# Late key/value units at the start of a causal attention stage, the next stage's first unit at its end, and logits placed behind the values

## The chip, the cores and the metric

One core of a Trainium2 chip runs the whole kernel. The metric is the device time of one execution in microseconds (us). TensorE (PE) multiplies matrices, VectorE (DVE), ScalarE (ACT) and GpSimd (POOL) do the rest, and SyncE (SP) starts most DMAs. Each engine works through its own instructions in program order and waits on semaphores.

## The reference

The kernel computes a two-layer decoder on x of shape (32, 128, 256) with a context of the same shape. Each sublayer is followed by a residual and a layer norm.

```python
x = _layernorm(x + _L0_attn_ref(x, ...))              # gated linear recurrence
x = _layernorm(x + _L0_xattn_ref(x, ctx_1024, ctx_1024, Wq, Wk, Wv))   # retention, decay mask
x = _layernorm(x + _L0_ffn_ref(x, wg, w1, b1, w2, b2))   # 8 experts, top 2, capacity
x = _layernorm(x + _L1_attn_ref(x, wq, wk, wv, wo))      # causal attention, 2 heads, rope
x = _layernorm(x + _L1_xattn_ref(x, ctx_1024, mask, ...))  # 16 heads over ctx, key mask
x = _layernorm(x + _L1_ffn_ref(x, hasher_w, keys, values_down, values_up, scale))
```

The last attention needs `K = ctx @ Wk + bk` and `V = ctx @ Wv + bv` of all 32 sequences. The router of the expert layer needs `logits = xt @ wg` of all tokens before any expert starts.

## The kernel before, in words

The 32 sequences are worked in 16 units of two (`UNITS` = 16, T = 256 tokens). The program is a row of stages. In each stage every engine runs the same `step(t)`, and `t.at(k, UNITS)` gives the unit that is k steps behind, so one step works on several units at different depths. The order of work on an engine is thus written out by hand in `step`. `pipelined` peels the first and last steps and loops the ones in between; its argument `first` names the first step that runs.

- **Stage A** (`a_tensor`, `a_scalar`, `a_vector`, `a_gpsimd`, `a_sync`; steps 0 to 20): recurrence, retention and router logits. In a step TensorE does, among others, the scaled scores' product with the values (line 673, which waits for VectorE's line 833), the query projection (622), the transposes of x2 (495), the logits (690, from the copy x2F that ScalarE makes in line 758), the values projection of the unit two steps younger (698) and the transposes of the context (495). The transposed context of each unit is stored in `cF_d`.
- **Router and early keys/values** (`kv_project`, `r_vector`): keys and values of units 0 to 8 (`KV_FIRST` = 9) are projected while VectorE computes the routing.
- **Stage M** (`m_*`; 16 tiles of 512 slots): the experts. It starts with gathers of token rows by GpSimd (line 1159). At its end `run_layer` closes the block: all engines meet at a barrier, after `m_end` on SyncE has waited for the last store of y.
- **Late keys/values** (`kv_rest_tensor`, `kv_rest_scalar`, lines 1353 to 1376): units 9 to 15 (`KV_REST` = 7). SyncE loads their seven context tiles after the barrier (1357); TensorE projects keys (line 503, 8 matmuls) and values (line 511, 8 matmuls) of each; ScalarE copies both banks out (1373) and starts the store into `kv_d` (1376). All that stands ahead of step 0 or step 2 of the next stage on TensorE and ScalarE, and TensorE then waits until the last copy is done.
- **Stage C** (`c_tensor`, `c_scalar`, `c_vector`, `c_gpsimd`, `c_sync`; steps 0 to 20): causal attention. GpSimd gathers four blocks of expert rows a unit (1432); VectorE mixes them with x2 and takes statistics (1617, 455); GpSimd takes the root (1412); ScalarE writes x3 (1421). TensorE turns x3 in step u+2 (495), projects queries (1472), keys (1472) and values (1527), makes the scores in step u+3 (1498, 1504), and in step u+4 transposes the probabilities (1486), multiplies with the values (1519) and projects out (1535). SyncE loads the key mask (line 1392) in step 0, and the first two units of stage E in step 16.
- **Stage E** (`e_*`; steps 0 to 17): sixteen-head attention. For the unit one step behind, `scores_and_less` makes two quads of scores at a time (1855, 1868), `less_max` takes their maxima on VectorE (2051), `turn_max` turns these (1888), and then the same scores are made again, transposed and with the maximum subtracted (1862, 1877), for `exps` on ScalarE (1968). `e_turn` and `e_query` (495, 503) and `e_keys` (1825, four copies on ScalarE) prepare a unit. Unit 0's turn and query stand in step 18 of stage C, its keys in step 19. Its scores come in stage E's step 1, and step 2 is the first with all parts.
- **Stage D**: the last feed-forward part, untouched.

## Time and profile before

| | us |
|---|---|
| median of 3 runs | 1602.99 (1600.58 to 1610.22) |
| the profiled execution, its own time | 1600.43 |
| its span in the trace | 1598.7 |

The profile is of one execution. The page gives each engine's busy share of the span: PE 93%, DVE 70%, ACT 51%, POOL 37%. Times in rows are microseconds from the start of the span. "PEclk" is the granted TensorE clock as a share of full speed (1.00 is 2.4 GHz, 0.50 is 1.2 GHz). In a timeline row the first number is the start, the second the duration; "x8" is eight instructions merged; what stands in brackets is the idle time of that engine before the row and what ended it. The stages lie at: A 0 to 250, router 250 to 299, M 299 to 677, late keys/values 683 to 713, C 713 to 910, E 910 to 1165, D from there.

### The profile page before, as it was taken

The page shows a single profiled execution, that of the slowest core. Times are in us where ns is not written, and L with a number is a line of the kernel's source. Part 1 is how long each engine was busy: PE and PEld are TensorE (multiplying, and loading weights), DVE is VectorE, ACT ScalarE, POOL GpSimd, SP SyncE. Part 2 cuts the span into 40 slices and gives each one's busy share as a digit, 9 for nine tenths or more (in the row PEclk, how much of TensorE's full clock was granted, in tenths as well). Part 3 has the DMA queues.
Part 4 walks back from the last instruction along what each step waited for, and adds up shares of the span by engine and source line. Part 5 has one row for each costly group of instructions (what it writes and reads, how often), then busy time and mean ns, then how long its engine had stood idle before and what let it go on. Part 6 is the DMA issues. An engine that isn't in the chain of part 4 may idle for free.

```text
span 1598.7 us, 34301 instructions
## 1 busy us (share of the span) xinstructions
PE 1479.5 (93%) x12682; PEld 1332.2 (83%) x12682; DVE 1113.4 (70%) x2303; ACT 819.1 (51%) x1559; POOL 583.5 (37%) x684
## 2 busy tenths in 40 slices
PE   5889989899999999978999799999979999999997
PEld 3777877799999999867778678888879999989997
DVE  3899988646655655317888468888767676868684
ACT  6777742344543454325777556656534444444442
POOL 2655540312111210037887213313124444444443
PEclk9999999899999999988999889999989999999999
DMA  6222253221323321062333124222136445454633
GB/s 209 73 80 79 72 184 132 68 74 57 104 95 105 105 95 38 14 220 76 91 94 108 59 92 134 82 66 70 36 78 126 103 101 114 91 117 85 127 77 67
DMA packets 118151, 151.97 MB, mean 95 GB/s; under 512 B 10090, under 2 KB 102852, under 8 KB 117508
## 3 DMA queue, kind: packets, MB, share of 16 engines
q1 hardware_dynamic: 110068, 127.48, 28.9%
q0 software_dynamic: 6560, 19.02, 4.2%
q10 hardware_dynamic: 1392, 3.70, 0.6%
q8 instruction: 85, 1.39, 0.4%
q14 instruction: 46, 0.38, 0.1%
HBM read 111.37 MB, written 38.80 MB: 94 GB/s over the span
## 4 chain that ended last, share of the span: by engine, by line
PE 31%; DVE 8%; issue 6%; DMA 5%; POOL 3%; ACT 2%; SPq 1%; DVEq 0%; POOLq 0%; ACTq 0%
PE psum L536 10%; PE psum L1900 4%; DMA arena_x<-wT_d 3%; PE psum L503 3%; PE psum L511 3%; PE psum L1877 2%; PE psum L1868 2%; DVE psum L2487 2%; PE psum L1472 2%; POOL arena_y L1432 1%; PE psum L1855 1%; PE psum L1862 1%; DMA wT_d<-arena_w 1%; SPq L2231 1%; PE psum L495 1%
## 5 line engine op out<-in xcount | busy, mean ns | idle before, releaser
L2258 POOL TENSOR_TENSOR d_g_parts<-arena_w,d_g_parts 128x512 fp32r<-128x512 f32 x128 | 166.5, 1301 | 241.4 <-ACT d_g_parts L2390 236.3
L536 PE MATMUL psum<-d_v_high,d_g_parts 128*128 128x256 f32 x1024 | 205.3, 284 | 4.8 <-POOL d_g_parts L2258 2.4
L536 PE MATMUL psum<-d_x_parts,d_v_high 128*128 128x256 f32 x1024 | 193.7, 287 | 1.3 <-DVE d_x_parts L531 1.3
L536 PE MATMUL psum<-m_w_high,m_h_parts 128*128 128x256 f32 x1024 | 188.0, 285 | 0.0
L1231 ACT ACTIVATE arena_x<-psum,b_e 128x512 f32<-128x512 f32 x128 | 88.3, 690 | 189.8 <-PE psum L536 88.8
L1159 POOL DMA_INDIRECT arena_x<-x_d,slot_row x64 | 66.7, 1043 | 293.6 <-PE psum L1205 229.4
L536 PEld LDWEIGHTS psum<-d_v_high,d_g_parts 128*128 128x128 f32 x1024 | 168.5, 192 | 5.9 <-issue 4.6
L536 PEld LDWEIGHTS psum<-d_x_parts,d_v_high 128*128 128x128 f32 x1024 | 159.3, 192 | 8.2 <-DVE arena_w L2493 5.3
L536 PE MATMUL psum<-m_xF_parts,m_w_high 128*128 128x512 f32 x512 | 159.9, 394 | 2.1 <-DVE m_xF_parts L531 2.1
L536 PEld LDWEIGHTS psum<-m_w_high,m_h_parts 128*128 128x128 f32 x1024 | 160.9, 192 | 0.0
L536 PE MATMUL psum<-d_vu_low,d_g_parts 128*128 128x256 f32 x512 | 145.4, 284 | 0.0
L536 PE MATMUL psum<-m_w_low,m_h_parts 128*128 128x256 f32 x512 | 145.1, 283 | 0.0
L536 PE MATMUL psum<-d_x_parts,d_vd_low 128*128 128x256 f32 x512 | 144.9, 283 | 0.0
L2398 ACT ACTIVATE arena_y<-psum 128x512 f32<-128x512 f32 x128 | 75.9, 593 | 119.6 <-PE psum L536 118.5
L2487 DVE SCALAR_TENSOR_TENSOR psum<-arena_y,psum 128x512 f32<-128x512 f32 x128 | 88.3, 690 | 68.8 <-ACT arena_y L2398 68.5
L2390 ACT ACTIVATE d_g_parts<-arena_w 128x512 fp32r<-128x512 f32 x128 | 80.5, 629 | 106.0 <-DVE arena_w L2493 106.0
L2493 DVE TENSOR_TENSOR arena_w<-psum,arena_x 128x512 f32<-128x512 f32 x128 | 88.5, 691 | 38.2 <-DMA arena_x<-wT_d 33.7
L531 DVE TENSOR_TENSOR m_h_parts<-arena_x,m_h_parts 128x512 fp32r<-128x512 f32 x128 | 84.7, 688 | 43.2 <-ACT m_h_parts L1235 43.2
L536 PEld LDWEIGHTS psum<-m_xF_parts,m_w_high 128*128 128x128 f32 x512 | 96.2, 190 | 21.7 <-issue 2.5
L1968 ACT ACTIVATE arena_x<-psum,arena_x 128x1024 f32<-128x1024 f32 x64 | 71.2, 1112 | 58.4 <-PE psum L1877 56.2
L536 PE MATMUL psum<-m_xF_parts,m_w_low 128*128 128x512 f32 x256 | 100.5, 393 | 0.0
L536 PEld LDWEIGHTS psum<-m_w_low,m_h_parts 128*128 128x128 f32 x512 | 98.4, 192 | 0.0
(284 smaller groups left out, 3699.3 us busy)
## 6 DMA issues: line engine op xcount, KB each, us to landing
arena_x<-wT_d SPq DMA_DIRECT2D x128, 256.0 KB, 5.7
arena_y<-in_L_ffn_w SPq DMA_DIRECT2D x16, 1024.0 KB, 8.0
x_d<-arena_x SPq DMA_DIRECT2D x32, 256.0 KB, 2.2
y_d<-arena_x SPq DMA_DIRECT2D x16, 512.0 KB, 9.0
arena_x<-kv_d SPq DMA_DIRECT2D x16, 512.0 KB, 3.5
kv_d<-arena_x SPq DMA_DIRECT2D x9, 512.0 KB, 2.8
arena_x<-in_x SPq DMA_DIRECT2D x16, 256.0 KB, 2.9
arena_x<-in_ctx SPq DMA_DIRECT2D x16, 256.0 KB, 3.1
```

What stands on the lines that cost most here:

```text
L503: ins = nc.tensor.matmul(dst[:, m * T:(m + 1) * T], w[name][:, c, m * P:(m + 1) * P], src[:, c, :], start=(c == 0), stop=(c == NC_ - 1))
L531: return nc.vector.tensor_tensor(dst, src, high.bitcast(F32), ALU.subtract)
L536: ins = nc.tensor.matmul(dst, left[a_], right[b_], start=start and k == 0, stop=stop and k == 2, skip_group_check=True)
L1159: nc.gpsimd.indirect_dma_start(out=M["x"][:, u.p, q, :], out_offset=None, in_=x2_d.rearrange("b s d -> (b s) d"), in_offset=bass.IndirectO ...
L1231: nc.scalar.activation(M["hr"][:, m % 4, :], bank(2 + m % 4), ACT.Relu, bias=b1_e[:, (u.c // 2) % 2, m:m + 1]).then_inc(m_hs, 1)
L1900: ins = nc.tensor.matmul(bank(7)[32 * quad:32 * quad + 32, (kind * NC_ + c) * S:(kind * NC_ + c + 1) * S], left, X["eT"][:, b, at:at + S], ...
L1968: nc.scalar.activation(X["eT"][:, b, half * 1024:(half + 1) * 1024].rearrange("p (q n) -> p q n", q=2), psum[:, 4:6, :], ACT.Exp, scale=HD ...
L2258: nc.gpsimd.tensor_tensor(K["gP"][:, s % 4, 1], K["g"][:, s % 2], K["gP"][:, s % 4, 0].bitcast(F32), ALU.subtract).then_inc(d_gl, 1)
L2390: nc.scalar.activation(K["gP"][:, s % 4, 0], K["g"][:, s % 2], ACT.Copy).then_inc(d_gh, 1)
L2398: nc.scalar.activation(K["th"][:, s % 2], bank(2 + s % 4).rearrange("p (k t) -> p k t", k=2), ACT.Tanh, scale=0.5).then_inc(d_th, 1)
L2487: nc.vector.scalar_tensor_tensor(z, K["th"][:, s % 2].rearrange("p k t -> p (k t)"), 1.0, z, ALU.add, ALU.mult).then_inc(d_t, 1)
L2493: nc.vector.tensor_tensor(K["g"][:, s % 2], z, K["w"][:, s // 4, 2 * (s % 4):2 * (s % 4) + 2, :] .rearrange("p k t -> p (k t)"), ALU.mult) ...
```

## The change

**Logits behind the values.** In stage A's step TensorE now does the values (698) between the transposes of x2 and the logits (690); ScalarE copies the values out before the logits.

**Kept context tiles.** At the end of the router's part SyncE loads the seven context tiles into memory that stage M doesn't use (four places of the weights that only stage A needs, and three at the ends of two arenas). After stage M's last tile and ahead of the barrier TensorE makes the first three of the 14 halves (a half is the keys or the values of a unit: 8 matmuls and one bank).

**Late units spread over stage C's first steps.** TensorE makes halves 3 to 9 before the steps, 10 and 11 at the start of step 3, 12 and 13 in step 4. ScalarE copies halves 0 to 5 out first, 6 to 9 at the start of step 2 (behind step 1's x3 of unit 0), 10 and 11 in step 3, 12 and 13 in step 4, and starts one store at the head of each of steps 2 to 7, the seventh in step 7. The key mask is loaded in step 2 instead of step 0.

**Stage E's steps 0 and 1 in stage C's last steps.** Unit 0's turn, query and keys move to step 17, its scores to steps 18 and 19, as do the turn, query and keys of unit 1 and the turn of unit 2; stage E then begins at its step 2 (`first=2`). The helpers `scores_and_less`, `turn_max`, `values`, `exps`, `less_rows`, `less_max` and the values' preparation (now `e_values`) become functions of the stage, otherwise as they were.

```diff
@@ a_tensor @@
+                if u3:
+                    done(pe, a_r2, u3.back(1))
...
+                    ins.then_inc(a_v, 1)
+                if u5:
                     done(pe, a_x2F, u5)
                     if u4:
                         done(pe, a_sc, u4)
@@ a_scalar @@
+                if u3:
+                    done(act, a_v, u3)
+                    done(act, a_ret, u3.back(2))
+                    nc.scalar.activation(A["v"][:, u3.p], seqs(bank(6)), ACT.Copy).then_inc(a_vs, 1)
                 if u5:
                     done(act, a_logit, u5)
@@ r_sync @@
+            for s in (a_gate, a_q, a_k, a_v, a_r2, a_ret, a_sc):
+                sp.wait_ge(s, UNITS)
+            sp.wait_ge(ln2[3], UNITS)
+            for k in range(KV_KEPT):
+                sp.dma_start(cF_kept[k].rearrange("p c t -> p (c t)"), cF_d[KV_FIRST + k]).then_inc(kv_kept, 16)
@@ m_tensor @@
             pipelined(pe, TILES, 1, step, unroll=4, peel=4)
+            pe.wait_ge(kv_kept, 16 * KV_KEPT)
+            pe.wait_ge(m_hh, TILES * HC)
+            project_features(bank(2), "L1_xattn_Wk", cF_kept[0])
+            project_rows(bank(3), "L1_xattn_Wv", cF_kept[0])
+            project_features(bank(4), "L1_xattn_Wk", cF_kept[1])
@@ late units @@
+        HALF_BANK = (2, 3, 4, 5, 6, 7, 4, 5, 6, 7, 5, 6, 7, 6)
+        HALVES_MADE = 3
+        def kv_rest_tensor(pe, *halves):
+            for n in halves:
+                k, j = divmod(n, 2)
+                src = cF_kept[k]
+                if HALF_BANK[n] in HALF_BANK[:n]:
+                    pe.wait_ge(kr_s, max(m for m in range(n) if HALF_BANK[m] == HALF_BANK[n]) + 1)
...
+        def kv_rest_scalar(act, *halves):
...
+                nc.scalar.activation(KV["kv_rest"][:, k, j], bank(HALF_BANK[n]), ACT.Copy).then_inc(kr_s, 1)
@@ c_sync @@
-                if t.fixed and t.n < 2:
-                    for k in ((0, 1), range(2, KV_REST))[t.n]:
-                        kv_rest_load(sp, k)
...
-                if t.fixed and t.n == 0:
+                if t.fixed and t.n == 2:
                     sp.dma_start(X["mask_u8"], a["mask"].rearrange("(a b) s -> a (b s)", a=1)
...
+                if t.fixed and t.n == UNITS + 3:
+                    e_load(sp, D2)
@@ c_tensor @@
-            kv_rest_tensor(pe)
+            kv_rest_tensor(pe, *range(3, 10))
...
+                if t.fixed and t.n == 3:
+                    kv_rest_tensor(pe, 10, 11)
...
+                if t.fixed and t.n == 4:
+                    kv_rest_tensor(pe, 12, 13)
+                    pe.wait_ge(kr_s, 11)
...
+                if t.fixed and t.n == UNITS + 2:
+                    pe.wait_ge(x_one, 6)
+                    for part in (c_x3F, c_qt, c_q2):
+                        pe.wait_ge(part, UNITS)
+                    done(pe, x_qs, D0)
+                    done(pe, x_ks, D0, 4)
+                    done(pe, x_mask, D0)
+                    scores_and_less(pe, (D0, 0, 0), None)
...
+                if t.fixed and t.n == UNITS + 1:
+                    e_turn(pe, D0, 0)
+                if t.fixed and t.n == UNITS + 3:
+                    scores_and_less(pe, (D0, 1, 0), None)
...
+                if t.fixed and t.n == UNITS + 2:
+                    for part in (c_kt, c_k2, c_vs):
+                        pe.wait_ge(part, UNITS)
+                    scores_and_less(pe, (D0, 0, 1), None)
+                if t.fixed and t.n == UNITS + 3:
+                    for part in (c_ex, c_pTs):
+                        pe.wait_ge(part, UNITS)
+                    scores_and_less(pe, (D0, 1, 1), (D0, 0, 0))
...
+                if t.fixed and t.n == UNITS + 1:
+                    e_query(pe, D0, 0)
                 if t.fixed and t.n == UNITS + 2:
-                    e_query(pe, Unit(0, 0, 4), 1)
+                    e_turn(pe, D1, 6)
+                    turn_max(pe, D0, 0)
+                if t.fixed and t.n == UNITS + 3:
+                    e_query(pe, D1, 6)
+                    turn_max(pe, D0, 1)
+                    done(pe, x_qs, D1)
+                    e_turn(pe, D2, 6)
@@ c_scalar @@
-            kv_rest_scalar(act)
+            kv_rest_scalar(act, *range(6))
...
+                if t.fixed and 2 <= t.n < 8:
+                    kv_rest_store(act, t.n - 2)
+                if t.fixed and t.n == 2:
+                    kv_rest_scalar(act, 6, 7, 8, 9)
...
+                if t.fixed and t.n == UNITS + 3:
+                    done(act, x_mkey, D0)
+                    exps(act, D0, 0, 0)
+                    e_take_query(act, D1, 6)
+                    e_take_turned(act, D2, 6)
+                    less_rows(act, D0, 1)
+                    e_keys(act, D1)
...
+                if t.fixed and t.n == UNITS + 1:
+                    e_take_query(act, D0, 0)
+                    e_keys(act, D0)
                 if t.fixed and t.n == UNITS + 2:
-                    e_take_query(act, Unit(0, 0, 4), 1)
-                if t.fixed and t.n == UNITS + 3:
-                    e_keys(act, Unit(0, 0, 4))
+                    e_take_turned(act, D1, 6)
+                    less_rows(act, D0, 0)
@@ c_vector (constants of stage E one step earlier, maxima and values of unit 0) @@
+                if t.fixed and t.n == UNITS + 2:
+                    less_max(dve, D0, 0, 0)
...
+                    e_values(dve, D0)
+                if t.fixed and t.n == UNITS + 2:
+                    less_max(dve, D0, 0, 1)
+                if t.fixed and t.n == UNITS + 3:
+                    less_max(dve, D0, 1, 0)
+                    less_max(dve, D0, 1, 1)
+                    e_values(dve, D1)
@@ e_sync, e_gpsimd, e_tensor, e_scalar, e_vector @@
-            pipelined(pe, UNITS, E_LAG, step, unroll=4, peel=4, tail=E_TAIL)
+            pipelined(pe, UNITS, E_LAG, step, unroll=4, peel=4, tail=E_TAIL, first=2)
```

## Rows read from the trace of the kernel before

**Rows 1.** Windows by stage: engines' busy us (instructions), then PEclk, DMA share, GB/s

```profile
60.00:210.00 150.00, 135.88 (x782) 119.92 (x782) 142.09 (x304) 116.42 (x210) 87.83 (x92) 1.00 0.29 93
...
677.30:715.20 37.90, 26.30 (x114) 22.62 (x113) 4.32 (x14) 8.69 (x16) 11.21 (x20) 0.86 0.63 220
715.20:747.60 32.40, 27.73 (x123) 23.01 (x124) 24.06 (x57) 15.62 (x42) 22.73 (x29) 0.84 0.24 75
747.60:880.80 133.20, 123.20 (x685) 105.78 (x684) 118.75 (x336) 98.62 (x263) 104.42 (x149) 1.00 0.34 99
880.80:928.00 47.20, 35.70 (x205) 28.63 (x203) 22.84 (x59) 25.22 (x65) 13.60 (x27) 0.83 0.13 45
```

**Rows 2.** Timeline of TensorE from stage M's end to stage C's step 5

```profile
677.03 0.28 PE L536 MATMUL psum<-m_w_high,m_h_parts 128*128 128x256 f32 x1
686.15 3.78 PE L503 MATMUL psum<-arena_x,arena_w 128*128 128x256 f32 x8 [8.84 <-DMA arena_x<-cF_d]
...
710.53 1.89 PE L511 MATMUL psum<-arena_w,arena_x 128*128 128x256 f32 x8
...
...
747.57 0.60 PE L495 MATMUL psum<-arena_w,arena_y 128*128 128x128 f32 x4
```

**Rows 3.** Timelines of GpSimd, VectorE and ScalarE between stages M and C

```profile
687.77 0.95 POOL L1432 DMA_INDIRECT arena_y<-y_d,c_idx_t  x1 [0.30 <-issue]
695.07 1.80 DVE L1617 SCALAR_TENSOR_TENSOR arena_y<-arena_y,gates 128x256 f32<-128x256 f32 x4 [16.43 <-DMA arena_y<-y_d,c_idx_t]
712.46 1.09 ACT L1373 ACTIVATE arena_x<-psum 128x512 f32<-128x512 f32 x2 [2.37 <-PE psum L511]
713.95 1.09 ACT L1421 ACTIVATE arena_y<-arena_y,C_st 128x256 f32<-128x256 f32 x2 [0.40 <-ACT arena_x L1373]
```

**Rows 4.** DMA view, issues by line: count, (KB,) median us to landing, 684 to 695

```profile
arena_y<-y_d,c_idx_t POOLq DMA_INDIRECT x5, 6.9
```

**Rows 5.** DMA view, 296 to 297 and 293 to 299, and TensorE's start of stage M

```profile
q1 hardware_dynamic: 79, 0.32, 102.4%
...
arena_x<-x_d,slot_row POOLq DMA_INDIRECT x5, 3.0
...
299.01 1.94 PE L1205 MATMUL psum<-arena_w,arena_x 128*128 128x128 f32 x8 [5.42 <-DMA arena_x<-x_d,slot_row]
```

**Rows 6.** Stage A: TensorE's wait for x2F (total, times, longest), then timeline rows

```profile
PE psum L690 <- ACT arena_x L758: 11.7, 16, 0.8
...
154.40 1.13 PE L673 MATMUL psum<-arena_x,arena_y 128*128 128x256 f32 x4 [0.76 <-DVE arena_y L833]
...
165.10 0.69 DVE L828 TENSOR_TENSOR arena_x<-arena_x 128x508 f32<-128x508 f32 x1
...
165.53 1.38 POOL L888 TENSOR_TENSOR arena_x<-arena_x 128x512 f32<-128x512 f32 x1 [3.82 <-ACT arena_x L729]
...
167.05 0.69 DVE L790 TENSOR_TENSOR arena_x<-psum,arena_w 128x512 f32<-128x512 f32 x1 [0.92 <-PE psum L622]
...
178.12 1.63 DVE L828 TENSOR_TENSOR arena_x<-arena_x 128x508 f32<-128x508 f32 x1
...
180.14 1.13 PE L673 MATMUL psum<-arena_x,arena_y 128*128 128x256 f32 x4 [0.77 <-DVE arena_y L833]
```

**Rows 7.** Timelines of TensorE and ScalarE from stage C's step 17 to stage E's step 3

```profile
890.65 1.89 PE L1535 MATMUL psum<-arena_w,arena_y 128*128 128x256 f32 x8
...
906.50 2.06 ACT L1825 ACTIVATE arena_x<-arena_x,kb_par,arena_w 128x256 f32<-128x256 f32 x4
...
911.91 1.04 PE L1868 MATMUL psum<-arena_x 32*128 32x256 f32 x8
...
927.99 0.61 PE L1855 MATMUL psum<-arena_x,mask_one 1*128 1x512 bf16 x2 [0.31 <-ACT arena_x L1968]
...
930.85 2.66 PE L503 MATMUL psum<-arena_x,L_xattn_Wq 128*128 128x256 f32 x8
...
945.66 1.99 PE L503 MATMUL psum<-arena_x,L_xattn_Wq 128*128 128x256 f32 x8
```

More of the change, by code:

```diff
@@ L693, in step @@
                     ins.then_inc(a_logit, 1)
-                if u3:
-                    done(pe, a_r2, u3.back(1))
-                    for b in range(UB):
-                        for c in range(NC_):
-                            ins = nc.tensor.matmul(bank(6)[:, b * D:(b + 1) * D],
-                                                   A["cF"][:, u3.p, c, b * S:(b + 1) * S],
-                                                   w["L0_xattn_Wv"][:, c, :], start=(c == 0), stop=(c == NC_ - 1))
-                    ins.then_inc(a_v, 1)
                 if u2:
@@ L1053, in decoder @@
         KV_FIRST = 9
+        KV_KEPT = UNITS - KV_FIRST
+        cF_kept = [w["L0_xattn_W" + n] for n in ("q", "k", "v")]
+        cF_kept.append(gate_w[:, :, :, :].rearrange("p g c n -> p g (c n)"))
+        arena_y.reset(13440)
+        cF_kept += [arena_y.take([P, NC_, T]) for _ in range(2)]
+        arena_x.reset(22528)
+        cF_kept.append(arena_x.take([P, NC_, T]))
+        kv_kept = sem("kv_kept")
         def kv_load(sp, u):
@@ L1516, in step @@
                     done(pe, c_os, u3.back(1))
+                    if t.fixed and t.n == UNITS + 3:
+                        done(pe, x_xF, D1)
+                    if t.fixed and t.n == 4:
+                        pe.wait_ge(kr_s, 2 * KV_REST)
                     for b in range(UB):
@@ new lines, in scores_and_less @@
+                            ins = nc.tensor.matmul(bank(4 + quad % 2)[:, j * S:(j + 1) * S],
+                                                   X["k"][rows, v.p, par, c * T + vb * S:c * T + (vb + 1) * S],
+                                                   X["q"][rows, v.c % 4, c, vb * S:(vb + 1) * S],
+                                                   start=False, stop=(j == 3), skip_group_check=True)
+            if sc:
+                got.then_inc(x_S, 1)
+            if less:
+                ins.then_inc(x_less, 1)
@@ new lines, in turn_max, with values @@
+        def turn_max(pe, u, b):
+            seq_done(pe, x_mx, u, b, 2)
+            nc.tensor.transpose(bank(3)[:, 0:P], X["mx"][:, b, :], ident).then_inc(x_mxT, 1)
+        def values(pe, u, b):
+            seq_done(pe, x_ex, u, b, 2)
+            seq_done(pe, x_at, u, b - 1)
+            for c in range(NC_):
+                for par in range(2):
+                    for kind in range(2):
+                        for quad in range(4):
+                            at = (4 * quad + 2 * c + par) * S
+                            left = (X["v"][:, u.p, b, 8 * c + 2 * quad + par, :], X["half"][:, par, :])[kind]
+                            ins = nc.tensor.matmul(
+                                bank(7)[32 * quad:32 * quad + 32, (kind * NC_ + c) * S:(kind * NC_ + c + 1) * S],
+                                left, X["eT"][:, b, at:at + S],
+                                start=(c == par == kind == 0), stop=(c == par == kind == 1), skip_group_check=True)
+            ins.then_inc(x_pv, 1)
@@ L1928, in step @@
                     done(pe, x_vs, u2)
[L1929 removed]
+                    values(pe, u2, 0)
                 if u1 and not u0:
```

271 lines of the change are left out of this document (123 added, 148 removed).

## The prediction

> **What bounds the kernel now.** I read the windows by stage first, since the page's 93% for TensorE is a mean. TensorE is busy 93% of a stage C step, but only 69% of the stretch between stage M and stage C's first turn, 86% of C's first steps and 76% of the seam between C and E, at a granted clock of 0.83 to 0.86 [rows 1]. Those three stretches are what the change edits, and in them the chain of waits runs over TensorE, its inputs and the barrier. In stage A the highest share is VectorE's, 142.1 of 150 us [rows 1], so there the question is who waits for whom.
>
> **The start of C.** Next, TensorE's timeline. M's last matmul ends at 677.3. The next starts at 686.15, after 8.84 us, for a context tile loaded behind the barrier. Its eight matmuls take 3.78 us where the last eight take 1.89, so the clock had fallen to 1.2 GHz [rows 2]. Starts follow each other by 1.73 us at full clock (the first tile's slow half apart, 14 halves end at 712.4). ScalarE, held in the same order, gives x3 of unit 0 only at 713.95, though its statistics began at 695.07 [rows 3]. Step 5 begins at 747.57 [rows 2].
>
> New order. The barrier stays near 683.1: it hangs on SyncE and the y store, and the three halves made ahead of it (3 x 1.73 = 5.2 us from 677.3) end at 682.5, inside that wait. If SyncE's wait weren't there they would cost 5.2; as it is, nothing. Halves 3 to 9 take 7 x 1.73 = 12.1, to 695.3, at full clock, because TensorE has just worked.
>
> Meanwhile x3 of unit 0. Before, its gather, issued at 687.77, held VectorE until 695.07 [rows 3], for a landing of 6.9 us [rows 4]. That was beside seven context loads and the mask, which are gone from here. A gather in a lighter queue lands in 3.0 [rows 5]. So 690.8; the mix, statistics, root and x3 take what stands between 695.07 and VectorE's and GpSimd's next work, some 4 us, plus 1.1 for x3 [rows 3]: 695.9. TensorE and x3 meet within 1 us. ScalarE then copies four halves (4 x 0.55, from 1.09 for two [rows 3]) ahead of the copy of x3's turn: 2.2 plus 0.6, queries from 698.9. Everything behind ScalarE's four copies waits for that, and it is about 2 us of idle TensorE.
>
> Step 2 has q, k and v, 5.2 us, to 704. Step 3 has two halves, turn, q, scores, k, v: 3.5 + 0.5 + 0.7 wait + 5.2 + 1.1 = 11.0, to 715. Step 4 has the full 10 us of a steady step (93% of 11.1 [rows 1]), two halves (3.5) and the waits for copies, about 15, to 730. The probabilities of unit 0 come 7 to 8 us behind its scores; halves 12 and 13 now lie in that wait, at full clock. 747.6 - 730 = 17.4 gained. Against it: the stores that ScalarE now starts at the head of steps 5 to 7, about 0.35 us each ahead of a copy that TensorE waits for, 1 us. The term is **-16.5**. Least: x3's chain and ScalarE's copies hold every step to 13 or more, -9. Most: TensorE without a gap after 683.1 has 19.0 for 11 halves and 22.5 for steps 2 to 4, 724.6, so -23.
>
> **The price in stage M.** The same seven loads, 1.8 MB, now start at about 295.2, right behind the last key/value store, and M's first tile waits for the last of its four gathers, landing at 299.0 [rows 5]. The row shows what a full direct queue does: from 296 to 297 q1 moved 79 packets at 102% and GpSimd's q0 none [rows 5]. At C's start the same loads stretched landings from 3.0 to 6.9 [rows 4, 5]. From this I take **+3**, with bounds 0 and +4. Stage M is otherwise bound by TensorE, so this isn't won back.
> The Trainium skill ("DMA: Bandwidth & Descriptors", Queues, rings and completion order) says that each DMA engine takes turns between its queues, a packet at a time. By that rule the gather would lose little, and the sum would be about 2 us lower; the row with no q0 packet speaks against it, and I follow the row.
>
> **Stage A.** TensorE waits 11.7 us in 16 waits for x2F before the logits [rows 6]. The values, 1.7 us, now cover that copy. But TensorE isn't alone. Two steps take 25.74 us (154.40 to 180.14), 12.87 each. In that pair TensorE waits once for VectorE's decayed scores (0.76), and VectorE once for TensorE's keys (0.92). VectorE's line 828 takes 0.69 when it starts before GpSimd's line 888 (165.10 against 165.53) and 1.63 in the other step [rows 6].
> If TensorE runs 0.77 earlier, ScalarE and GpSimd's line 888 do too: about 10.35 us behind line 673 instead of 11.1. VectorE reaches line 828 10.7 to 11.0 after it. Then GpSimd goes first in every step. Line 828 ends 1.8 after GpSimd's start, line 833 0.35 later, and the next 673 follows: 10.35 + 1.8 + 0.35 + 0.05 = 12.55 a step. 0.31 x 14 steps with both parts gives **-4.3**. Bounds: -10.8 (all of 0.77 x 14) and +7 (each step as long as the longer one, 13.37). ScalarE's swapped copies cost nothing: the logits' copy isn't read in the stage.
> The Trainium skill ("SBUF — State Buffer", SBUF: two separate sides) calls the port that VectorE and GpSimd share an exclusive lock, held for a whole instruction. By that rule alone the collision costs VectorE up to the whole of GpSimd's instruction in each step, which is the third case below; the pair 0.69 and 1.63 agrees with it.
>
> **The seam from C to E.** Step 17 starts near 880.8 either way (less what came before). Its last matmuls end at 892.5; stage E's step 2 begins at 927.99 [rows 7], 35.5 later. New: a turn (0.45) and query (1.75) lengthen step 17 to 894.6, with its query copy (0.8) and the four key copies (2.06 [rows 7]) ScalarE is done at 897.6, and TensorE waits 2.5 us there: the keys' copies also hold the next probabilities' copy. Then, at full clock, in program order: scores 1.3 (1.04 and the mask pair [rows 7]), C scores 1.1, values product 0.9, scores 1.3, projection 1.75, turn 0.45, a wait for the maxima: 904.7. Step 19: 0.45 + 1.3 + wait and 0.9 + four-quad scores 1.7 + projection 1.75 + query 1.75 + the two small turns, to 913.8. The query's copy, unit 2's turn and copy, the row copy and the keys put ScalarE at 917.5. Step 2 of E starts there: -10.5. Step 2 then took 14.8 from query to query, but its first query took 2.66 against 1.99 [rows 7]; the denser work ahead should leave less of it slow, -0.7. The term is **-11**. Bounds -4 (the clock is at 1.2 GHz for this seam too, and ScalarE's keys hold it) and -14. E's second step onward is as before: same order, same waits; unit 3's x4 load, now behind C's last store, is about 921, needed near 931.
>
> **Sum.** -16.5 + 3 - 4.3 - 11 = -28.8. From the profiled execution's 1600.4 that is 1571.6; from the shown median, 1603.0, 1574.2. I predict 1573. About 1% (16 us) is what a measurement of this kernel tells from no change.
>
> **Rivals.**
> 1. *VectorE keeps stage A.* GpSimd's earlier start makes line 828 long in every step and VectorE's cycle 13.0 (167.05 to 833's end, 180.1 [rows 6]): +2 instead of -4.3, 1580. For it: VectorE's 95% [rows 1]. Against: in that count VectorE also starts its long step late.
> 2. *C's first steps hang on the gathers and ScalarE.* One unit takes gathers, mix, root and x3 in turn. If each of steps 2 to 5 runs at 13 and the copies of halves push x3's turn back, the start gives 9 and the seam 6: 1603 - 9 + 3 - 4.3 - 6 = 1587. For it: VectorE is at 89% in steady C [rows 1].
> 3. *All covers hold.* Stage A gives 10.8, the gathers of M lose nothing, start and seam give 19 and 13: 1560. For it: rows 6's waits; against: VectorE's share.
> 4. *The clock stays at 1.2 GHz (slower than before).* The short bursts between waits don't bring it back. The start then takes 2 x (19.0 + 22.5) = 83 us from 683.1, ending at 766, +18.6; the seam's 13 us of work doubles, +2; M +3, A -4: 1622. It decides from the first gap of step 2 on. For it: 0.50 behind M, and 0.83 to 0.86 in all three stretches [rows 1]. Against: the second group of late halves already ran at full clock, and the gaps get shorter here.
>
> **Chances.** Forecast 0.60, rival 1 0.17, rival 2 0.10, rival 3 0.10, rival 4 0.03. The forecast's own terms move by some 7 us together, 1566 to 1581. For 8 in 10 I go into rivals 1 to 3: 1561 to 1587. Faster by over 1% (under 1587): all but rival 4 and half of rival 2, 0.92; within 1%: 0.05; slower: 0.03.
>
> **What would show it.** The rest of M's block ends with three groups of 8 matmuls right behind 677; the barrier isn't later. Line 1373 has no row ahead of the first x3, and TensorE's first turn of C comes near 696, its step 5 near 730 (with A's and M's shifts taken out). Rows of 8 matmuls take 1.9, not 3.8. M's first transposes wait 8 us instead of 5.4. In A the wait of line 690 for x2F is gone and line 828 is long in nearly every step. From step 17's last projection to E's step 2 there are 25 us instead of 35.5. The forecast is wrong if the step of C or of E gets longer, if the first turn of C comes after 702, or if the steps of A aren't shorter.

## The result, and the profile after

| | us |
|---|---|
| kernel before, median of 4 runs | 1602.92 (1600.58 to 1610.22) |
| changed kernel, median of 4 runs | 1582.74 (1579.31 to 1587.21) |
| ratio | 0.9872, 95% interval [0.9835, 0.9908] |
| profiled execution after | 1587.21, span 1585.4, granted clock 0.979 |

The change gains 20 us. I had forecast 29 (1573, range 1561 to 1587): the time lies within the range, the gain is 30% smaller. The profiled execution is the slowest of the four, and this matters below.

First the windows by stage of the changed kernel, the stretches of [rows 1] at their new places (busy us and instructions of TensorE, its weight loads, VectorE, ScalarE, GpSimd, then granted clock, DMA share, GB/s):

```profile
60.00:210.00 150.00, 138.43 (x794) 121.13 (x792) 146.56 (x307) 118.59 (x211) 95.76 (x94) 1.00 0.29 97
677.05:696.71 19.66, 17.67 (x83) 14.93 (x81) 4.29 (x13) 4.51 (x9) 7.80 (x14) 1.00 0.41 129
696.71:731.11 34.40, 30.46 (x154) 25.62 (x155) 23.79 (x57) 19.21 (x50) 25.23 (x35) 1.00 0.40 126
731.11:864.38 133.27, 123.23 (x685) 105.62 (x684) 118.81 (x336) 99.03 (x264) 105.85 (x150) 1.00 0.38 115
864.38:905.74 41.36, 33.63 (x202) 27.36 (x201) 22.94 (x58) 24.82 (x65) 13.53 (x27) 0.87 0.12 39
```

The stretch from M's last matmul to C's first turn fell from 37.9 to 19.7 us, at full clock instead of 0.86. C's steady part takes 133.3 us, as before. The seam is still at 0.87, against 0.83.

TensorE's timeline of the changed kernel from M's end to C's step 5, answering to [rows 2]:

```profile
677.05 1.89 PE L503 MATMUL psum<-arena_w 128*128 128x256 f32 x8
...
680.50 1.89 PE L503 MATMUL psum<-arena_w 128*128 128x256 f32 x8
683.84 1.97 PE L511 MATMUL psum<-arena_w 128*128 128x256 f32 x8 [1.45 <-PEq L368]
...
694.28 1.89 PE L511 MATMUL psum<-arena_w,arena_y 128*128 128x256 f32 x8
696.71 0.66 PE L495 MATMUL psum<-arena_w,arena_y 128*128 128x128 f32 x4 [0.54 <-ACT arena_y L1444]
...
731.11 0.60 PE L495 MATMUL psum<-arena_w,arena_y 128*128 128x128 f32 x4
```

Every group of eight takes 1.9 to 2.0 us; the slow half of 3.78 is gone. The first turn comes at 696.71 (forecast 695.9 to 696), step 5 at 731.11 (forecast 730). The timelines of GpSimd and VectorE, answering to [rows 3]:

```profile
683.83 0.18 POOL L1466 COPY c_idx_t<-slot_g 128x4 int32<-128x4 int32 x1 [81.08 <-POOLq L368]
...
691.30 1.80 DVE L1698 SCALAR_TENSOR_TENSOR arena_y<-arena_y,gates 128x256 f32<-128x256 f32 x4 [12.76 <-DMA arena_y<-y_d,c_idx_t]
```

And the DMA view between 684 and 695 (count, median us to landing), answering to [rows 4]:

```profile
arena_y<-y_d,c_idx_t POOLq DMA_INDIRECT x5, 2.8
```

Without the context loads beside them the gathers land in 2.8 us instead of 6.9. The same seven loads now meet stage M's first gathers. The DMA view between 294 and 299, then TensorE's start of M, answering to [rows 5]:

```profile
arena_x<-x_d,slot_row POOLq DMA_INDIRECT x4, 6.0
```

```profile
298.58 1.94 PE L1219 MATMUL psum<-arena_w,arena_x 128*128 128x128 f32 x8 [8.29 <-DMA arena_x<-x_d,slot_row]
```

Landing 6.0 instead of 3.0, the wait 8.29 instead of 5.42: 2.9 us paid, 3 forecast.

Stage A, answering to [rows 6]: TensorE's wait for x2F in the view of waits (us in total, times, longest), then timeline rows of one step:

```profile
PE psum L699 <- ACT arena_x L759: 1.4, 2, 0.7
```

```profile
192.16 1.13 PE L673 MATMUL psum<-arena_x,arena_y 128*128 128x256 f32 x4 [0.69 <-DVE arena_y L834]
195.29 1.89 PE L689 MATMUL psum<-arena_w,arena_x 128*128 128x256 f32 x8
197.02 0.95 PE L699 MATMUL psum<-w_route,arena_x 128*128 128x8 f32 x8
202.88 1.57 DVE L829 TENSOR_TENSOR arena_x<-arena_x 128x508 f32<-128x508 f32 x1
204.84 1.13 PE L673 MATMUL psum<-arena_x,arena_y 128*128 128x256 f32 x4 [0.69 <-DVE arena_y L834]
```

The 11.7 us of waiting are 1.4. Yet a step still takes 12.68 us here, 12.78 in the mean (64.28 to 204.84 is 11 steps) against 12.88: TensorE now waits for VectorE in each step, not in every other. VectorE's line 828 (829 in this kernel) has a duration of 1.57 or 1.58 us in all twelve steps from 62 to 204, where it was long in seven of twelve before.

The seam, answering to [rows 7]: TensorE from the first wait for the key copies to E's step 3, then three windows:

```profile
881.01 0.39 PE L1941 MATMUL psum<-arena_x,mask_one 1*128 1x512 bf16 x2 [2.65 <-ACT arena_x L1916]
...
883.40 1.91 PE L1544 MATMUL psum<-arena_y 128*128 128x128 f32 x8
...
889.19 3.15 PE L1589 MATMUL psum<-arena_w,arena_y 128*128 128x256 f32 x8
...
905.74 0.61 PE L1941 MATMUL psum<-arena_x,mask_one 1*128 1x512 bf16 x2 [3.18 <-issue]
...
908.60 3.68 PE L503 MATMUL psum<-arena_x,L_xattn_Wq 128*128 128x256 f32 x8
...
921.57 3.64 PE L1986 MATMUL psum<-arena_x 128*32 128x128 f32 x64
...
926.09 0.39 PE L1941 MATMUL psum<-arena_x,mask_one 1*128 1x512 bf16 x2
```

```profile
881.00:891.00 10.00, 9.99 (x41) 7.69 (x42) 3.49 (x5) 4.60 (x16) 0.73 (x2) 0.52 0.08 28
...
903.00:912.20 9.20, 6.46 (x42) 5.19 (x42) 1.23 (x1) 4.41 (x9) 1.20 (x4) 0.63 0.45 138
...
918.70:925.20 6.50, 6.44 (x99) 5.63 (x99) 1.64 (x2) 3.04 (x5) 2.19 (x6) 0.51 0.05 19
```

E's step 2 begins 22.25 us earlier than before (927.99), but step 3 only 18.0 (944.13 before), while step 17 had already been 16.4 earlier. So in this execution almost nothing of the seam's 11 us is left, and the rows show why it can't be the work: the same eight small matmuls (line 1544; 1504 before) take 1.91 instead of 1.05 us, a projection 3.2 to 3.7 instead of 1.9. After each of three pauses (2.65, 3.18, and one of 1.26 ahead of the row at 918.76) TensorE stands at its lower level, 1.2 GHz, for a while.

### The profile page after: what moved, and what is told of

It is laid out like the page before. It is cut to its first block, busy times and chain, and to the rows that moved or that the text cites. A ratio compares the mean times of both kernels' runs of the same rounds, so it can differ in the third digit from the quotient of the medians.

```text
span 1585.4 us, 34297 instructions
## 1 busy us (share of the span) xinstructions
PE 1478.6 (93%) x12682; PEld 1328.5 (84%) x12682; DVE 1116.0 (70%) x2303; ACT 820.8 (52%) x1559; POOL 591.3 (37%) x684
## 4 chain that ended last, share of the span: by engine, by line
PE 34%; DVE 7%; issue 6%; DMA 4%; POOL 2%; ACT 2%; SPq 1%; DVEq 0%; POOLq 0%; ACTq 0%
PE psum L536 12%; PE psum L1986 4%; DMA arena_x<-wT_d 2%; PE psum L1963 2%; PE psum L1954 2%; PE psum L503 2%; PE psum L511 2%; PE psum L1497 2%; DVE psum L2575 1%; PE psum L1589 1%; PE psum L1941 1%; PE psum L1948 1%; POOL d_g_parts L2346 1%; DMA wT_d<-arena_w 1%; PE psum L495 1%
## 5 line engine op out<-in xcount | busy, mean ns | idle before, releaser
L531 DVE TENSOR_TENSOR m_h_parts<-arena_x,m_h_parts 128x512 fp32r<-128x512 f32 x128 | 84.6, 687 | 43.6 <-ACT m_h_parts L1254 43.6
```

What stands on the lines that cost most here:

```text
L531: return nc.vector.tensor_tensor(dst, src, high.bitcast(F32), ALU.subtract)
```

## The experiments

Theory: the seam's gain was given back because TensorE's pauses there, above all the two for ScalarE's key copies, let its clock fall. Rivals: the new order of the seam is a serial chain and costs it anyway; or the profiled execution was an accident. "After" below is the changed kernel. The kernel before was run again beside them: 1603.48 us beside runs 1 to 4, 1603.42 beside 5 to 8, 1601.70 beside 9 to 12. Ratios and intervals are against that; differences in us are between medians unless it is said otherwise. "The distance" is the time from C's first turn to E's step 3.

**1. The changed kernel again** (no edit).

> The changed kernel once more, unaltered, as the base of the three runs beside it. Its profiled execution on record was the slowest of its four (1587.21 against 1579.31 us). If the fall of TensorE's clock in the seam is a property of the program, the granted clock is at 0.5 to 0.6 again from about 881 to 891 us and from about 903 to 912 us, and E's third step begins within 1 us of 926. If it was an accident of that one execution, both stretches stand near 1.0 and the third step begins 5 to 9 us earlier (917 to 921). Time: 1579 to 1587 us.

1582.38 us (1580.07 to 1586.20), 0.9867 [0.9853, 0.9881]. Its windows:

```profile
881.00:891.00 10.00, 7.36 (x44) 5.75 (x43) 4.67 (x15) 6.14 (x18) 0.91 (x2) 0.83 0.08 28
...
903.00:912.20 9.20, 6.03 (x43) 5.01 (x42) 1.23 (x1) 4.81 (x9) 1.27 (x4) 0.63 0.48 147
912.20:918.70 6.50, 5.37 (x134) 4.66 (x133) 4.05 (x4) 3.31 (x6) 0.00 (x0) 1.00 0.80 311
```

Between the two cases: the second fall is there again at 0.63, the first is short, the third is missing. From C's first turn (699.29) to E's step 3 (922.95) it takes 223.7 us; the recorded execution took 229.4, the next run 223.5. The two waits for the key copies are the same (2.64 and 3.17 us), so the same program meets the falls at different cost. I use this distance as the measure of the seam from here.

One more pause differs, and the forecast had no term for it. Ahead of unit 2's turn in step 19 TensorE waits 0.82 us for the query's copy in the record, and here for unit 2's new load:

```profile
902.46 0.63 PE L495 MATMUL psum<-arena_w,arena_x 128*128 128x128 f32 x4 [1.71 <-DMA arena_x<-kv_d]
```

It is 1.71 us here, 1.87 in run 2 and 1.72 in run 7, and 0.82 in runs 4, 5, 6 and 10 to 12. So 0.9 us of run 1's distance is this load. Run 6, without it, has a distance of 223.3.

**2. Stage A's order put back.**

```diff
@@ a_tensor, and the two copies in a_scalar likewise @@
                     to_feature(bank(0), A["x2"][:, u5.p]).then_inc(aT_x2, 1)
-                if u3:
-                    done(pe, a_r2, u3.back(1))
...
-                    ins.then_inc(a_v, 1)
-                if u5:
                     done(pe, a_x2F, u5)
...
                     ins.then_inc(a_logit, 1)
+                if u3:
+                    done(pe, a_r2, u3.back(1))
...
+                    ins.then_inc(a_v, 1)
```

> The changed kernel with stage A's order put back (logits ahead of the values on TensorE and ScalarE). By the row of the last logits, which moved from 246.56 to 243.28 us, the order is worth 3.3 us: the last logits are back within 1 us of 246.6, and the time is 3 to 4 us above the changed kernel's. Rival: what the order gains is taken back at the router or at stage M's first gathers, which wait for something else; then the time is within 1 us of the changed kernel's although the last logits move.

1584.38 us, 0.9882 [0.9866, 0.9897]: +2.0, where 3 to 4 were expected. The last logits are at 246.82. The sign is as expected; the interval overlaps that of run 1.

**3. The seam put back.**

```diff
@@ c_tensor; c_sync, c_gpsimd, c_scalar and c_vector likewise @@
-                if t.fixed and t.n == UNITS + 1:
+                if t.fixed and t.n == UNITS + 2:
                     e_turn(pe, D0, 0)
-                if t.fixed and t.n == UNITS + 3:
-                    scores_and_less(pe, (D0, 1, 0), None)
...
-                if t.fixed and t.n == UNITS + 1:
-                    e_query(pe, D0, 0)
+                if t.fixed and t.n == UNITS + 2:
+                    e_query(pe, D0, 1)
@@ e_tensor and the other four of stage E @@
-            pipelined(pe, UNITS, E_LAG, step, unroll=4, peel=4, tail=E_TAIL, first=2)
+            pipelined(pe, UNITS, E_LAG, step, unroll=4, peel=4, tail=E_TAIL)
```

> The changed kernel with the seam from the causal attention to the sixteen heads' stage as it was before; stage A, the kept tiles and C's start stay changed. By the ledger of the one profiled execution the seam brings 1.6 us: the time is 1 to 3 us above the changed kernel's and E's third step begins 1.6 us later (about 927.6). By my forecast it would bring 11: the time is 10 to 12 us above. If the clock's fall inside the seam is what eats the rest, the granted clock here stands near 1.0 in the stretches from 881 to 891 and from 903 to 912 us where TensorE is busy, or falls in other places as it did in the kernel before.

1588.91 us, 0.9913 [0.9899, 0.9928]: +6.5. First turn to E's step 3 takes 230.7 us (697.81 to 928.49), 7.0 more than in run 1. So the seam brings 6.5 to 7, neither the recorded 1.6 nor the forecast 11. The old seam stands at low clock too (0.64 from 891 to 903): the falls aren't new, and the new order removed only some of them. From the end of step 17's last projection to E's step 3 the granted clock is 0.80 in the kernel before and in this run, 0.88 in runs 1 and 6, and 0.76 in the record.

**4. The key copies ahead**, in ScalarE's pauses before the attention's output copy.

```diff
@@ c_scalar @@
+                if t.fixed and t.n == UNITS + 1:
+                    e_keys(act, D0)
+                if t.fixed and t.n == UNITS + 2:
+                    e_keys(act, D1)
                 if u3:
                     done(act, c_o, u3)
...
                     e_take_query(act, D0, 0)
-                    e_keys(act, D0)
...
                     less_rows(act, D0, 1)
-                    e_keys(act, D1)
```

> The changed kernel with ScalarE's key copies of the first two units moved ahead, into the two pauses in which ScalarE waits for the attention's outputs in C's last steps (3.3 and 4.1 us long; the copies take 2.06 us). Theory (the two waits of 2.65 and 3.2 us for the copies let the clock fall, and the fall costs more than the waits): both waits go, the granted clock of 881 to 891 us and of 903 to 912 us rises from 0.52 and 0.63 to above 0.9, E's third step begins 8 to 11 us earlier (915 to 918 instead of 926), and the time is 8 to 11 us below the changed kernel's. Rival A (the seam's serial order costs it, the clock only follows the idle time): the waits are taken up by the next link of the chain (the query's copy, the maxima), the clock still falls, and the time is 0 to 3 us below. Rival B: only the waits themselves are won, with no clock effect: 4 to 5 us below, the clock unchanged.

1574.38 us (1562.95 to 1581.13), 0.9815 [0.9786, 0.9844]: 8.0 below run 1. TensorE's rows and the windows:

```profile
879.39 0.39 PE L1943 MATMUL psum<-arena_x,mask_one 1*128 1x512 bf16 x2 [0.80 <-ACT arena_x L1909]
...
885.80 1.97 PE L1589 MATMUL psum<-arena_w,arena_y 128*128 128x256 f32 x8 [1.86 <-ACT arena_y L1645]
...
898.37 0.39 PE L1943 MATMUL psum<-arena_x,mask_one 1*128 1x512 bf16 x2
...
908.39 0.39 PE L1943 MATMUL psum<-arena_x,mask_one 1*128 1x512 bf16 x2 [1.26 <-issue]
```

```profile
881.00:891.00 10.00, 7.92 (x58) 6.20 (x57) 5.47 (x14) 7.43 (x22) 1.52 (x3) 1.00 0.08 26
891.00:903.00 12.00, 11.10 (x132) 9.31 (x133) 5.78 (x13) 7.10 (x13) 5.14 (x14) 1.00 0.41 133
903.00:912.20 9.20, 7.94 (x171) 7.01 (x171) 5.76 (x5) 5.58 (x8) 2.19 (x6) 0.82 0.85 317
```

The wait ahead of step 18's scores is 0.80 instead of 2.64, the one ahead of E's step 2 gone, though 1.86 came up at the output projection, since in step 18 the copies now lie ahead of the copy it needs. The distance is 217.1 us, 6.6 less than run 1 (8 to 11 expected for E's third step). This doesn't separate wait from clock; runs 5 and 10 do.

**5. Matmuls that compute nothing in the two waits**; the waits themselves and every order stay (the loop stands twice, with 8 and 12).

```diff
@@ c_tensor @@
                     done(pe, x_qs, D0)
+                    for _ in range(8):
+                        nc.tensor.matmul(bank(0)[:, 0:D], w["L1_xattn_Wq"][:, 0, 0:P],
+                                         w["L1_xattn_Wq"][:, 0, :], start=True, stop=True)
                     done(pe, x_ks, D0, 4)
```

> The changed kernel with matmuls that compute nothing put into TensorE's two waits for the key copies (8 of 128x256 into the free bank 0 in step 18, 12 in E's second step's wait; 0.24 us each at full clock, so they fit into the waits). The waits and every order stay. If the clock falls because TensorE pauses there, the granted clock from 903 to 912 us rises from 0.63 to above 0.9, E's third step, which begins 223.6 us after C's first turn in the repeated run, begins about 217 to 221 us after it, and the time is 3 to 6 us below the changed kernel's, with no wait taken away. If the wait itself is the cost and the clock follows something else, the third step stays at 223 to 225 us and the time within 1.5 us (or above it, where the filler delays the next instruction).

1577.68 us, 0.9849 [0.9831, 0.9866]. The price of one was wrong in my expectation (0.46 us, not 0.24: each counts as two instructions in a row, 8 of them as x16): the two groups took 3.7 and 5.4 us and ended after the waits.

```profile
881.00:891.00 10.00, 9.42 (x60) 7.61 (x60) 4.70 (x15) 6.12 (x19) 0.91 (x2) 1.00 0.08 28
...
903.00:912.20 9.20, 9.20 (x100) 7.70 (x102) 1.50 (x2) 4.73 (x9) 0.69 (x3) 1.00 0.60 183
```

The clock is at 1.00 in both, and although the overhang delays E's step 2 (207.7 us after the first turn, 204.0 in run 10 with the short filling), step 3 comes 221.9 us after the first turn instead of 223.7: E's step 2 takes 14.1 us instead of 16.7. That is less than expected (217 to 221), and the interval of the time overlaps that of run 1.

**6. The kept tiles loaded in stage M's fourth step.**

```diff
@@ r_sync, m_sync @@
-            for k in range(KV_KEPT):
-                sp.dma_start(cF_kept[k]...).then_inc(kv_kept, 16)
...
+                if t.fixed and t.n == 3:
+                    for k in range(KV_KEPT):
+                        sp.dma_start(cF_kept[k]...).then_inc(kv_kept, 16)
```

> The changed kernel with the loads of the kept context tiles moved from the end of the router stage into the expert stage's fourth step. If these loads are what slows the first gathers (wait of 8.1 to 8.4 us ahead of the expert stage's first transposes, against 5.4 before), the wait is back at 5.3 to 5.6 us and the time 2.5 to 3 us below the changed kernel's. Rival: the wait is the gathers' own and only the kernel's earlier start makes it look longer; then it stays above 7.5. Rival: the loads meet the expert weights' loads and pieces instead, and what is won at the start is lost by a wait within the expert stage (its 377 us grow by 1 to 3).

1578.29 us, 0.9843 [0.9829, 0.9856]: 4.1 below run 1. TensorE's first transposes of M:

```profile
296.55 1.94 PE L1220 MATMUL psum<-arena_w,arena_x 128*128 128x128 f32 x8 [5.50 <-DMA arena_x<-x_d,slot_row]
```

The wait is back at 5.5, and from there to C's first turn it takes 398.05 us as in the changed kernel (398.13), so the loads cost nothing within M. The price was in the gathers' company. The time fell by more than the wait did (8.09 to 5.50, 2.6 us; 2.5 to 3 were expected); where the other 1.5 lie isn't shown.

**7. No half ahead of the barrier.**

```diff
@@ m_tensor, late units, c_tensor @@
-            project_features(bank(2), "L1_xattn_Wk", cF_kept[0])
-            project_rows(bank(3), "L1_xattn_Wv", cF_kept[0])
-            project_features(bank(4), "L1_xattn_Wk", cF_kept[1])
...
-        HALVES_MADE = 3
+        HALVES_MADE = 0
...
-            kv_rest_tensor(pe, *range(3, 10))
+            kv_rest_tensor(pe, *range(0, 10))
```

> The changed kernel with none of the three late halves ahead of the barrier: they follow it, with the other seven. If they are hidden ahead of the barrier but for 0.7 to 0.9 us (barrier at 683.8 against 683.1), the barrier comes 0.7 to 0.9 us earlier, and the ten halves now end 5 us later than the seven did, so that C's first turn waits for TensorE and not for the first mix: it comes 4 to 5.5 us later and the time is 3.5 to 5 us above the changed kernel's. Rival: the first mix's gathers set the start anyway and the turns catch up by the fifth step; then the time is within 1 us.

1587.19 us, 0.9885 [0.9865, 0.9905]: 4.8 above run 1 by the medians, 2.9 by the ratios, and the intervals overlap. The first turn comes 403.7 us after M's first transposes instead of 398.1, so 5.5 late; the query of step 17 is 2.1 late (580.2 against 578.1 in run 1). The first steps win 3 us back. By E's step 3 it is only 1.0 late (623.2 against 622.2), with a distance of 219.5. What the medians show beyond that lies behind E's step 3 in these two executions (663.8 us to the end against 661.4), in parts that the edit doesn't touch. Its timeline at the barrier:

```profile
681.86 3.75 PE L503 MATMUL psum<-arena_w 128*128 128x256 f32 x8 [5.94 <-PEq L368]
```

From M's last matmul to the barrier it takes 5.9 us here as before, and 6.6 with the three halves. There they end at 682.39, and TensorE goes on 1.45 us later (the row of 683.84). I infer that it had become the last to arrive, which cost 0.7; no row shows who arrived last. The row also shows what the halves save besides their own time: after a pause of 5.94 us the first eight matmuls take 3.75 us again, at 1.2 GHz.

**8. The kernel before with stage A's new order alone** (run 2's diff the other way round, on the kernel before).

> The kernel before with stage A's new order alone (logits behind the values on TensorE and ScalarE). The profiled executions with the new order have the last logits at 243.3 to 245.7 us, those with the old one at 246.6 and 246.8: so 1 to 3.3 us are won, 2.5 by the means, and the time is 2 to 3 us below the kernel before's. Rival: what is won is lost again at the router, the time is within 0.5 us. My forecast's term was 4.3 us.

1599.76 us, 0.9978 [0.9969, 0.9987]: 3.7 won, 2 to 5 by the interval (2 to 3 expected). All profiled executions agree on where: 11 steps take 140.5 us in the new order and 141.7 in the old, and from the line 673 that ends them (near 205 us) to the last logits it is 38.4 or 39.4 against 40.8. From the first line 673 to the last logits that makes 2.6 to 2.7 us in some executions (run 8's own among them) and 3.4 to 3.6 in the others.

**9. Only the kept tiles and C's start** (edits 2 and 3 together).

> The changed kernel with stage A's order and the seam both as before: what is left of the change is the kept tiles with their loads and the late units in C's start. The terms measured so far (new order of A 3.7 us alone on the kernel before, seam 6.5 us undone, loads 4.1 us or, by the wait ahead of the transposes, 2.8) leave 10.9 to 11 us for this part of the 21.1 in all: expected 1592 to 1593 us, 10 to 12 us below the kernel before. My forecast for it was 16.5 - 3 = 13.5 us. If the parts don't add up (if they give clock to or take clock from one another), it differs from 11 by more than 3 us.

1590.75 us, 0.9935 [0.9912, 0.9957]: 10.95 below the kernel before, as expected. With 3.7 for A and 6.5 for the seam that makes 21.1, what run 1 shows. Up to E's step 3 (931.45, M's first transposes at 302.67) it is 16.3 us shorter than before (944.13 and 299.01), less 2.8 for M's longer wait: 13.6 unrounded, my forecast's 13.5. In these two executions 2.4 are lost after E's step 3 (656.95 us to the end, before 654.6), which is about what is missing.

**10. The filling half as long** (4 and 6).

> The matmuls that compute nothing once more, half as many (4 and 6), since the first filling took 3.7 and 5.4 us and so was 1.6 and 1.9 us longer than the waits that it filled; now 1.85 and 2.8 us, which end before the waits do. Theory (pauses of TensorE in the seam are what lets the clock fall): the clock from 903 to 912 us stays above 0.9, E's third step begins 217.5 to 220 us after C's first turn (223.6 without filling, 221.9 with the long one), and the time is 4 to 6 us below the changed kernel's 1582.4, at most 1577.7. Rival: the long filling helped only since it is dense enough; with the short one the clock falls again in part and the third step begins at 221 to 224.

1573.69 us (1566.41 to 1582.70), 0.9830 [0.9789, 0.9871]. TensorE around the second wait, and the windows:

```profile
899.42 2.75 PE L1607 MATMUL psum<-L_xattn_Wq 128*128 128x256 f32 x12
902.76 0.39 PE L1948 MATMUL psum<-arena_x,mask_one 1*128 1x512 bf16 x2 [0.58 <-issue]
```

```profile
903.00:912.20 9.20, 8.52 (x175) 7.28 (x169) 4.83 (x5) 4.30 (x7) 0.00 (x0) 1.00 0.86 288
912.20:918.70 6.50, 5.92 (x109) 5.24 (x111) 2.97 (x3) 3.63 (x7) 2.17 (x6) 0.74 0.32 122
```

Both waits are still there (the filling ends 0.58 ahead of the scores), both at full clock, and E's step 2 begins 24.8 us after step 17's last projection (877.99) instead of 27.4 in run 1, of which 0.9 is the load of unit 2. One fall is left, behind the pause of 1.26; step 3 comes after 219.8, 3.9 less than in run 1 and 3.5 less than in run 6, which had no wait for the load. The median is 8.7 below run 1's (5.9 by the ratios, and the intervals overlap), more than the profiles show, and the runs scatter over 16 us. That the clock holds the seam back is shown by the rows: but for the filling, the seam's order and waits are those of run 6. How much it brings in the mean isn't settled; 3 to 9 us.

**11 and 12. The two better edits together, and with five matmuls that compute nothing in the two pauses left** (three ahead of the wait for the output copy in step 18, into bank 7; two ahead of the fourth scores of E's step 2, into bank 6).

```diff
@@ c_tensor @@
                     done(pe, c_r4, u3.back(1))
+                    for _ in range(3 if t.fixed and t.n == UNITS + 2 else 0):
+                        nc.tensor.matmul(bank(7)[:, 0:D], ...)
                     done(pe, c_os, u3)
@@ e_tensor @@
+                if t.fixed and t.n == 2:
+                    done(pe, x_qs, u0)
+                    for _ in range(2):
+                        nc.tensor.matmul(bank(6)[:, 0:D], ...)
                 scores_and_less(pe, u1 and (u1, 1, 1), u1 and (u1, 0, 0))
```

> The two edits that each beat the changed kernel, together: the key copies moved ahead, and the kept tiles loaded in the expert stage. Alone they brought 8.0 and 4.1 us. If they add up, 1569 to 1572 us; if the clock takes part of the sum back, 1573 to 1575 us.

> The same with five matmuls that compute nothing, in TensorE's two remaining pauses of the seam (1.86 us ahead of the attention's output projection in step 18: three; 1.26 us ahead of the last logits in E's second step: two). With the keys ahead the granted clock was 1.00 to 903 us and 0.82 from 903 to 912 us, after the second of these pauses. If the pauses cause that, it is above 0.95 there and the third step begins 2 to 3 us earlier than without filling (217.1 us after C's first turn with the keys ahead); the time is 1 to 3 us below the kernel without filling. Rival: a pause of 1.3 us is too short to matter and the clock's level there depends on the time passed since an earlier fall; then nothing changes (within 1 us).

Run 11: 1574.59 us, 0.9841 [0.9811, 0.9870]. Its rows show both gains (M's wait 5.40, distance 217.1), but the median is no better than run 4's. Run 12: 1567.70 us (1559.82 to 1570.21), 0.9782 [0.9749, 0.9814], the lowest median of all; its interval barely meets run 11's. Its windows, at full clock through the whole seam:

```profile
891.00:903.00 12.00, 11.11 (x159) 9.43 (x161) 6.04 (x13) 6.66 (x12) 3.22 (x9) 1.00 0.60 190
903.00:912.20 9.20, 9.00 (x189) 7.52 (x182) 6.75 (x7) 5.15 (x10) 2.17 (x6) 1.00 0.62 241
```

The distance is 215.7, 1.4 less (2 to 3 expected). The median fell by 6.9, where 1 to 3 were expected, and most of that isn't located: run 11's profiled execution is the fastest of its six (1569.17), run 12's took 1567.93, and from E's step 3 to the end they take 657.6 and 655.6 us. What the clock does much later is seen in the same 55 us at the passage from E to D, in runs 9, 1 and 12, one line each:

```profile
1135.20:1190.20 55.00, 44.58 (x475) 40.22 (x468) 33.65 (x80) 18.19 (x34) 11.30 (x11) 0.88 0.34 77
```

```profile
1126.80:1181.80 55.00, 43.43 (x451) 37.74 (x441) 32.22 (x78) 16.19 (x30) 9.93 (x9) 0.84 0.28 64
```

```profile
1114.30:1169.30 55.00, 44.87 (x496) 40.32 (x489) 34.21 (x81) 18.65 (x35) 12.53 (x11) 0.94 0.38 83
```

From ScalarE's last copy of a turned x4 to its ninth tanh of stage D these three take 82.7, 86.0 and 80.2 us. No edit touches this part.

## Why the prediction was right or wrong

**The start of C, -16.5: right.** Step 5 came 16.5 us earlier in the record; counted from M's first transposes, which takes A's and M's shifts out, 16.0 (15.5 in run 1), and E's step 3 16.3 in run 9. The landings (3.0 forecast, 2.8), the first turn, the full clock and the 34.4 us to step 5 are as worked out. (747.6 less 730 is 17.6 and not 17.4, which changes nothing.) One assumption inside it was off: the three halves were not free. Their end looked covered (682.5 against 683.1), but TensorE goes on only 1.45 us behind it, and 0.7 came through. Run 7 shows that they are worth it all the same: 2.1 us at step 17, 3 to 5 in the time, which is not clear of the noise.

**The price in M, +3: right.** 2.9 in the record, 2.6 by the waits of runs 1 and 6 (4.1 by their medians). That the gather would lose little was my reading of the Trainium skill's rule that a DMA engine takes turns between its queues ("DMA: Bandwidth & Descriptors", Queues, rings and completion order). The landing went from 3.0 to 6.0, so the row decides against that reading; a doubling beside one full queue doesn't speak against the turns themselves.

**Stage A, -4.3: the size nearly, the working not.** 3.7 by run 8, 2.6 to 3.6 by rows. Line 828 is long in every step, as forecast, but the step is 12.78, not 12.55: 0.1 a step, 1.2 in the 11 steps measured. The other 1.4 to 2.3 came behind them, mostly in the drain, which I had not counted. That the size came near is luck in part. The first rival had the right bottleneck (TensorE waits for VectorE in each step) at too high a price. The exclusive port that the Trainium skill describes ("SBUF — State Buffer", SBUF: two separate sides) agrees with line 828's length in every step, but here it took back most of the gain and no more.

**The seam, -11: this step failed; 6.5 by run 3.** I had written "Then, at full clock, in program order". The waits were as forecast (2.65 against 2.5), and with the clock held by the filling of run 10 E's step 2 began 24.8 us after step 17's last projection, against a forecast of 25; without it 27.4 (0.9 of it the load of unit 2) and 29.7. The distance of run 10 is 10.9 us below run 3's, the forecast's 11. So the sum of the work was right and the clock not: a pause forecast at 2.5 us was priced at 2.5 us, but behind it everything took up to twice as long. The -0.7 for E's second step went the other way: 16.7 us in run 1 against 16.1 before, and 14.1 with the clock held (run 12). My fourth rival carried the clock's fall, but as a state of whole stretches that decides over the sign; it acts in bites of a few us behind single pauses.

**After the seam: 2.4 us or more given back.** From E's step 3 to the end the kernels run the same instructions, and took 654.6 us before, 655.1 in run 8, 656.95 in run 9, 661.4 in run 1, and between 650 and 664 in all. Some of it goes with the clock at the passage to D: 82.6 to 83.5 us where the window shows 0.88, 84.6 to 86.0 at 0.84, 85.6 to 86.7 at 0.81, 80.2 at 0.94. The seam as before mostly had 0.88, the new one mostly 0.84 or less, though the record's execution of the same program as run 1 had 0.88; whether and how an earlier change moves it stays open, and so does the rest of the scatter, which lies in stage D (395.2 us before, 395 to 401 in most runs, 387 in run 5).

**The sum.** Forecast 28.8, measured 21.1: seam 4.5 less, A 0.6 less, and 2.5 less for the start with its loads, which had been there up to E and was lost behind it. 1573 as a time is met by run 10, the changed kernel with most of its clock held, which is where the forecast's assumption was. That it is met so closely is luck: the parts measured one by one, with 3.9 for the filling, add up to 25 us and not 28, and run 10's profiled execution took 1577.

## What to carry to other kernels

Price a pause of TensorE between short bursts not by its length alone: look at the granted clock of the stretch behind it, and take the matmuls' durations there from rows at the lower level. Where such a pause can't be closed, first move the late producer's work into its own idle time (the key copies, 8 us), and then try a few matmuls into a free bank that end before the wait does (3.5 to 3.9 us here by the rows). When loads move to an earlier stage, ask which gather they will share the queues with; the same loads three tiles later cost nothing.

## What was not expected of the hardware

The clock fell behind pauses that differ little in length, and not always: behind 2.65 us in the record (0.52 for the next 10 us) but only shortly in run 1 behind 2.64; behind a pause of 1.26 us in the record and in runs 4, 10 and 11, and not in runs 1, 2, 5, 6 and 7. With useless matmuls in the pauses it stayed at 2.4 GHz each time (runs 5, 10 and 12). The Trainium skill ("TensorE: Matmul & The Clock Gate", Part 1: The HAM clock gate) says that activity of the array releases the throttle; that work without a result serves as well as any agrees.

What the clock does 200 us behind the seam, in a passage that no edit touches, differs by 5.4 us between the profiled executions of runs 11 and 12. Whether the edit moved it isn't shown: the record and run 1, one program, differ by 2.5 us there (83.5 and 86.0). Kernels that differ by less than that can't be ranked by one profile.
